# Attention and gated FFN in one kernel: q and k rows stacked by direct transfers between partitions, without a copy in memory

## The reference

```python
xn = layernorm(x)                       # x: (4, 512, 256), 4 batches
q, k, v = (xn @ W.T).reshape(B, T, 16, 16).transpose(0, 2, 1, 3) for W in (Wq, Wk, Wv)
w = softmax(causal(q @ k.T / sqrt(16)))
s = (w @ v).transpose(0, 2, 1, 3).reshape(B, T, 256) @ Wo.T
h = silu(xn @ Wg.T) * (xn @ Wu.T)       # 704 hidden, integer weights, zero point 128, a scale per row
g = silu(h @ Wd.T)
out = x + s * g
```

## Time and profile before

| | |
|---|---|
| median of 3 runs | 336.36 us (335.95 to 337.09) |
| profiled execution | 337.07 us |
| its span, first to last instruction | 335.2 us |
| TensorE / VectorE / ScalarE / GpSimd busy | 291.8 / 208.7 / 173.8 / 126.7 us |
| mean granted TensorE clock | 0.929 of full |
| moved by DMA | 31.41 MB, mean 94 GB/s |

### The profile page before, as it was taken

The page is one execution under the profiler, slowest core; times in us unless marked ns, Lnnn a source line. Parts: engine busy times, 40 slices in busy tenths (PEclk is TensorE's granted clock), DMA queues, the critical chain, the costliest instruction groups (busy, mean ns, idle before and its releaser), DMA issues.

```text
span 335.2 us, 5853 instructions
## 1 busy us (share of the span) xinstructions
PE 291.8 (87%) x2076; PEld 210.7 (63%) x2076; DVE 208.7 (62%) x714; ACT 173.8 (52%) x252; POOL 126.7 (38%) x227
## 2 busy tenths in 40 slices
PE   8798575999719999995997999999987999989983
PEld 8687443885515775892565666779553667747752
DVE  4994819686326866754385468494763699882305
ACT  3556327135426578931545464962661656774451
POOL 5108514043213679230215544450323366732130
PEclk9899958799978999997898599999999799998999
DMA  7936896006959000069266000025594400120001
GB/s 275 262 101 177 198 154 135 2 6 176 156 171 178 14 4 0 3 171 183 92 150 157 9 6 0 4 66 171 121 200 109 94 3 3 66 65 2 5 0 63
DMA packets 21632, 31.41 MB, mean 94 GB/s; under 512 B 2772, under 2 KB 10580, under 8 KB 21604
## 3 DMA queue, kind: packets, MB, share of 16 engines
q1 hardware_dynamic: 21188, 30.40, 38.5%
q10 hardware_dynamic: 416, 0.66, 0.5%
HBM read 20.20 MB, written 10.49 MB: 92 GB/s over the span
## 4 chain that ended last, share of the span: by engine, by line
PE 54%; DMA 23%; SPq 9%; DVE 7%; ACT 4%; issue 2%; POOL 0%; ACTq 0%; DVEq 0%
DMA qk_scratch<-hid 14%; PE ps L422 11%; PE ps L563 9%; PE ps L424 9%; PE ps L423 9%; PE ps L546 6%; PE ps L526 5%; DMA qp<-ctr 3%; SPq L372 3%; DMA qk_scratch<-xr 2%; DVE ps L976 2%; DMA kp<-qk_scratch 2%; ACT pt L760 2%; PE ps L573 2%; DMA pt<-in_woT 2%
## 5 line engine op out<-in xcount | busy, mean ns | idle before, releaser
L976 DVE CUSTOM_DVE_ANT_0 ps<-ps,maskt 128x512 f32<-128x512 f32 (+3 forms) x256 | 118.2, 521 | 38.7 <-PE ps L526 38.7
L824 POOL TENSOR_SCALAR_AFFINE_SELECT pt<-pt 128x256 f32<-128x256 f32 (+1 forms) x112 | 47.9, 443 | 127.3 <-ACT pt L760 126.2
L760 ACT ACTIVATE pt<-ps 128x1024 f32<-128x1024 f32 x80 | 79.9, 1028 | 23.3 <-PE ps L546 16.1
L546 PE MATMUL ps<-qp,kp 50*128 50x512 f32 (+3 forms) x256 | 37.0, 369 | 17.8 <-DVE hid L955 7.4
L526 PE MATMUL ps<-kp,qp 48*128 48x512 f32 (+3 forms) x256 | 36.3, 363 | 12.5 <-DMA kp<-qk_scratch 8.2
L800 POOL TENSOR_TENSOR hid<-hid 128x512 f32<-128x512 f32 x24 | 30.8, 1282 | 33.8 <-ACT hid L708 23.3
L422 PE MATMUL ps<-xh,guh 128*128 128x512 f32 x88 | 41.4, 470 | 2.1 <-DVE hid L955 2.1
L563 PE MATMUL ps<-pt,vt 128*32 128x256 f32 (+3 forms) x528 | 41.5, 458 | 1.7 <-POOL pt L824 1.5
L546 PEld LDWEIGHTS ps<-qp,kp 50*128 50x128 f32 x256 | 21.6, 196 | 31.0 <-issue 13.5
L700 ACT ACTIVATE hid<-ps,hsg 128x512 f32<-128x512 f32 (+1 forms) x24 | 16.4, 685 | 42.1 <-DMA qk_scratch<-hid 21.6
L526 PEld LDWEIGHTS ps<-kp,qp 48*128 48x128 f32 x256 | 21.9, 196 | 24.8 <-issue 21.5
(11 more groups left out here) (112 smaller groups left out, 482.5 us busy)
## 6 DMA issues: line engine op xcount, KB each, us to landing
qk_scratch<-hid SPq DMA_DIRECT2D x24, 256.0 KB
qp<-qk_scratch SPq DMA_DIRECT2D x14, 256.0 KB, 4.9
kp<-qk_scratch SPq DMA_DIRECT2D x14, 256.0 KB, 5.7
qp<-qk_scratch SPq DMA_DIRECT2D x18, 128.0 KB, 5.3
kp<-qk_scratch SPq DMA_DIRECT2D x18, 128.0 KB, 5.7
xr<-in_x SPq DMA_DIRECT2D x4, 512.0 KB, 4.5
out<-xr SPq DMA_DIRECT2D x8, 256.0 KB, 2.2
xin<-in_x SPq DMA_DIRECT2D x3, 512.0 KB, 7.7
```

The lines of the kernel that those rows point to most:

```text
L546: mm = nc.tensor.matmul(ps[:, banks[e], c:c + T - j * P], kp[part, place(b, half), col, j * P:(j + 1) * P], qp[part, place(b, half), col, ...
L760: nc.scalar.activation(pair(b, s), ps[:, b0:b1 + 1:b1 - b0, :], ACT.Exp, scale=SCALE).then_inc(exp_done, 1)
L824: mm = nc.gpsimd.affine_select(out=diag, in_=diag, compare_op=ALU.is_ge, fill=0.0, base=0, pattern=[[0, diag.shape[1]], [1, P]], channel_m ...
L976: mm = nc.vector.tensor_tensor_reduce(part, part, maskt[:, T - wide:], -1.0, TOP, ALU.add, ALU.min, mg[:, e, a // 2, i:i + 1])
```

## The change

The q and k weights are put in another column order, so that chunk g of `qk` is group g: 64 rows of q and 64 rows of k for four heads. From the staging tile, six DMAs between partitions write the stack at once: 64 staging partitions go to 32 partitions by two columns, each fourth partition of `qp` or `kp`. Of every four rows in `qp` three hold high, low, high, and in `kp` high, high, low; the fourth row is 0 in `qp` and 1 in `kp`. The rows of maxima go to partition 31 of every 32 in one DMA. All matmuls of both passes run over 64 rows. Since the first pass needs 0 where the second has the maxima, a DMA writes zeros there before a place is used again. `qp` and `kp` have 6 places of 4 heads, filled once by GpSimd. q and k get a staging tile `stg` of their own with two places, and the tanh no longer waits for transfers; `fth` is merged into `u` and `sdb` lies in `u`. `vt` is packed to 17 columns per head. The weights' split into high and low goes in three parts. All five orders are written anew.

```diff
-PAIRS = 6, ROWC = 3 * HD, KS = ROWC + 2
+PLACES = 6, VE = HD + 1
...
-            def store_qk(b, c):
-                half, which = c // 2, c % 2
-                w.need("qlo", qlo_done, 4 * b + c + 1)
-                if b >= 2:
-                    w.need(("pack", b % 2, half), pack_loaded[b % 2][half], 128 * (b // 2))
-                for s in range(2):
-                    sp.dma_start(qk_dram[b % 2, which, half, :, s], stage(b, c)[s]).then_inc(qk_stored[c], 16)
-
-            def stack_cols(b, half, which, cols, loaded):
-                w.need(("stored", 2 * half + which), qk_stored[2 * half + which], 32 * (b + 1))
...
+            def place_free(n):
+                if n < PLACES:
+                    w.need("rows", rows_set, 2 * (n + 1))
+                else:
+                    w.need("st", st_ready, 5 * (n - PLACES + 1))
+
+            def stack_hi(b, g):
+                n = NG * b + g
+                w.need("qhi", qhi_done, n + 1)
+                place_free(n)
+                if n >= PLACES:
+                    if n == PLACES:
+                        sp.wait_ge(ctr_zero, 1)
+                    sp.dma_start(qp[31::32, place(b, g)].bitcast(F32), ctr[:, 2, :].bitcast(F32)
+                                 ).then_inc(stacked[b % 2][g], 16)
+                hi = stage(b, g)[0]
+                for rows, src in ((qp[0::4], hi[0:64]), (kp[0::4], hi[64:P]), (qp[2::4], hi[0:64]), (kp[1::4], hi[64:P])):
+                    sp.dma_start(rows[:, place(b, g)].bitcast(F32), src.bitcast(F32)).then_inc(stacked[b % 2][g], 16)
+
+            def stack_lo(b, g):
+                n = NG * b + g
+                w.need("qlo", qlo_done, n + 1)
+                place_free(n)
+                lo = stage(b, g)[1]
+                for rows, src in ((qp[1::4], lo[0:64]), (kp[2::4], lo[64:P])):
+                    sp.dma_start(rows[:, place(b, g)].bitcast(F32), src.bitcast(F32)).then_inc(stacked[b % 2][g], 16)
 
             def c_rows(b, g):
                 n = NG * b + g
                 w.need("ct", ct_copied, n + 1)
-                for r in range(2):
-                    a = 2 * (g % 2)
-                    sp.dma_start(qp[64 * r + ROWC:64 * r + KS, place(b, g // 2), a:a + 2, :].bitcast(F32),
-                                 ctr[16 * r:16 * r + 16, n % 2, :].bitcast(F32)).then_inc(c_loaded[n % 2], 16)
+                sp.dma_start(qp[31::32, place(b, g)].bitcast(F32), ctr[:, n % 2, :].bitcast(F32)).then_inc(c_loaded[n % 2], 16)
...
             def chunk_hi(b, c):
                 w.need("qk", qk_ready, 4 * b + c + 1)
-                if b == 0 and c == 3:
-                    w.need("wl", wl_done, 2)
-                if b:
-                    w.need("hlo", hlo_done, HF * b)
-                    w.need("hlt", hlt_done, b)
                 if b and c >= 2:
-                    w.need(("stored", c - 2), qk_stored[c - 2], 32 * (b + 1))
-                nc.scalar.copy(stage(b, c)[0].bitcast(F32R), ps[:, bank_of("qk", b, c), :]).then_inc(qhi_done, 1)
+                    w.need(("stacked", b % 2, c - 2), stacked[b % 2][c - 2], stack_count(b, c - 2))
+                elif b:
+                    q, g = b - 1, (c if b == 1 else c + 2)
+                    w.need(("stacked", q % 2, g), stacked[q % 2][g], stack_count(q, g))
+                nc.scalar.copy(stage(b, c)[0], ps[:, bank_of("qk", b, c), :]).then_inc(qhi_done, 1)
...
             def gate_tanh(b, m):
                 w.need("gu", gu_ready, GUN * b + 2 * m + 1)
                 if m >= 2:
                     w.need("hlo", hlo_done, HF * b + m - 1)
+                elif b and m == 0:
+                    w.need("hlo", hlo_done, HF * b)
                 elif b:
-                    for c in (m, m + 2):
-                        w.need(("stored", c), qk_stored[c], 32 * (b + 1))
-                else:
-                    w.need("ones", kp_ones, 32)
+                    w.need("hlt", hlt_done, b)
...
+            def rows(_, n):
+                nc.gpsimd.memset(kp[:, n].bitcast(F32), 1.0).then_inc(rows_set, 1)
+                nc.gpsimd.memset(qp[:, n].bitcast(F32), 0.0).then_inc(rows_set, 1)
...
 TENSOR_ORDER (start)
-t:0:0:0 t:0:1:1 qk:0:0:0 qk:0:1:1 qk:0:2:2 qk:0:3:3 gu:0:0:0 gu:0:1:1 gu:0:2:2 gu:0:3:0 gu:0:4:1 gu:0:5:0 v:0:0:2
-m:0:0:01 m:0:1:34 m:0:2:56 v:0:1:7 m:0:3:01 gu:0:6:2 m:0:4:37 gu:0:7:4 m:0:5:56 gu:0:8:2 m:0:6:04 gu:0:9:1 gu:0:10:3
+t:0:0:0 t:0:1:1 qk:0:0:0 qk:0:1:1 qk:0:2:2 qk:0:3:0 gu:0:0:1 gu:0:1:3 gu:0:2:0 m:0:0:12 m:0:1:34 m:0:2:56 gu:0:3:7
+v:0:0:1 v:0:1:0 m:0:3:12 m:0:4:34 m:0:5:56 m:0:6:07 gu:0:4:1 gu:0:5:2 gu:0:6:3 c:0:0:1 gu:0:7:2 m:0:7:01 m:0:8:45
 SYNC_ORDER (after; units of batches 0 to 2)
+init4:0:0 loadx:1:0 pkh:0:0 pkl:0:0 pkl:0:1 pkh:0:1 pkh:0:2 pkl:0:2 pkh:0:3 pkl:0:3 loadres:0:0 crow:0:0 loadx:2:0
+crow:0:1 loadx:3:0 crow:0:2 pkh:1:0 pkl:1:0 pkh:1:1 pkl:1:1 crow:0:3 pkh:1:2 pkl:1:2 pkh:1:3 pkl:1:3 crow:1:0
+sout:0:0 sout:0:1 crow:1:1 loadres:1:0 crow:1:2 pkh:2:0 pkl:2:0 pkh:2:1 pkh:2:2 pkl:2:1 pkl:2:2 crow:1:3 pkh:2:3
 VECTOR_ORDER (start)
+init2:0:0 st:0:0 xn:0:0 xn:0:1 xn:0:2 xn:0:3 wlo:0:0 wlo:0:1 wlo:0:2 glo:0:0 xlo:0:0 xlo:0:1 wds:0:0 wol:0:0 bn:1:0
+wdl:0:0 qlo:0:0 qlo:0:1 bn:1:1 glo:0:1 qlo:0:2 qlo:0:3 bn:1:2 bn:1:3 gate:0:0 mom:1:0 maxa:0:0 maxb:0:0 maxa:0:1
```

More of the change, by code:

```diff
@@ L89 @@
+hhi:3:5 exp:3:4 fth:3:0 ccp:3:2 exp:3:5 zcp:3:0 exp:3:6 exp:3:7 exp:3:8 fth:3:1 exp:3:9 exp:3:10 ccp:3:3 exp:3:11
+exp:3:12 exp:3:13 zcp:3:1 exp:3:14 exp:3:15 exp:3:16 zhi:3:0 zcp:3:2 exp:3:17 exp:3:18 exp:3:19 zcp:3:3 zcp:3:4
+zhi:3:1 zhi:3:2
 """
 VECTOR_ORDER = """
-init2:0:0 st:0:0 xn:0:0 xn:0:1 xn:0:2 xn:0:3 wlo:0:0 glo:0:0 xlo:0:0 xlo:0:1 glo:0:1 wol:0:0 wds:0:0 qlo:0:0 qlo:0:1
-wlo:0:1 wdl:0:0 qlo:0:2 gate:0:0 qlo:0:3 bn:1:0 bn:1:1 bn:1:2 gate:0:1 bn:1:3 mom:1:0 gate:0:2 maxa:0:0 maxb:0:0
@@ L129 @@
+hid:3:0 mask:2:15 hlo:3:0 mask:2:16 mask:2:17 hid:3:1 mask:2:18 mask:2:19 hlo:3:1 hid:3:2 hid:3:3 hlo:3:2 hlo:3:3
+hid:3:4 hlo:3:4 mask:3:0 res:2:0 hid:3:5 mask:3:1 mask:3:2 mask:3:3 res:2:1 mask:3:4 mask:3:5 mask:3:6 mask:3:7
+mask:3:8 mask:3:9 mask:3:10 mask:3:11 mask:3:12 mask:3:13 mask:3:14 mask:3:15 mask:3:16 mask:3:17 mask:3:18
+mask:3:19
 """
 SYNC_ORDER = """
-init4:0:0 loadx:1:0 store:0:0 store:0:1 stackf:0:0 stackf:0:1 store:0:2 store:0:3 stack:0:0 stack:0:1 stack:0:2
-stack:0:3 loadres:0:0 loadx:2:0 crow:0:0 crow:0:1 store:1:0 store:1:1 stack:1:0 stack:1:1 loadx:3:0 store:1:2
@@ L409, in store_out @@
                              xr[:, 2 * n:2 * n + 2, :]).then_inc(out_stored, 16)
-            work = {"init4": load_first, "loadx": load_x, "loadres": load_residual, "store": store_qk,
-                    "stackf": stack_first, "stack": stack, "crow": c_rows, "sout": store_out}
+            work = {"init4": load_first, "loadx": load_x, "loadres": load_residual, "pkh": stack_hi, "pkl": stack_lo,
+                    "crow": c_rows, "sout": store_out}
             for kind, b, n, _ in SYNC:
@@ L513, in maxima @@
                 g, kk = divmod(m, 5)
-                half = g // 2
                 banks = take(("m", b, m))
-                if b == 0 and g == 0:
-                    w.need("first", first_pack, 128)
-                else:
-                    w.need(("pack", b % 2, half), pack_loaded[b % 2][half], 128 * (b // 2 + 1))
+                w.need(("stacked", b % 2, g), stacked[b % 2][g], stack_count(b, g))
                 both = [pair_blocks(kk, e) for e in range(2)]
@@ L524, in maxima @@
                         i = TT - 1 - j
[L525 to L527 removed]
+                        wide, part, col = (i + 1) * P, slice(64 * e, 64 * e + 64), a // 2
+                        mm = nc.tensor.matmul(ps[:, banks[e], c:c + wide], qp[part, place(b, g), col, i * P:(i + 1) * P],
+                                              kp[part, place(b, g), col, 0:wide], start=True, stop=True)
                 mm.then_inc(sm_ready, 1)
@@ L751, in exps @@
                 if n < PAIRS:
-                    w.need("wl", wl_done, 2)
+                    w.need("wl", wl_done, 3)
                     w.need("gul", gul_done, 2)
                     w.need("wol", wol_done, 1)
-                    for c in range(4):
-                        w.need(("stored", c), qk_stored[c], 32)
+                    w.need(("stacked", 0, 2), stacked[0][2], 96)
                 else:
@@ L849, in root @@
                     nc.gpsimd.tensor_scalar(shf[:], t, -1.0, None, ALU.mult).then_inc(shf_done, 1)
-            work = {"init3": constants, "sc": scales, "root": root, "mask": mask, "hid": hidden, "hlo": hidden_lo,
+            work = {"init3": constants, "rows": rows, "vones": value_ones, "sc": scales, "root": root, "mask": mask, "hid": hidden, "hlo": hidden_lo,
                     "res": residual}
```

295 lines of the change are left out of this document (133 added, 162 removed).

## The result

The change makes the kernel faster: 305.74 us (304.58 to 306.67) against 336.15 us before on the same chip, ratio 0.9096, 95% interval 0.9051 to 0.9142. That is 30.4 us; forecast were 18.2. The profiled execution's span is 304.9 us against 335.2.

A forecast was written before the change was run, and what follows sets the result against it. TensorE was taken as nearest the limit (busy 291.8 of 335.2 us), with 26.3 of its 43.4 idle us hanging on transfers, plus low clock. Terms summed to -18.2, from 337.1 to 318.9, stated as 318 us; range 302 to 336.

The forecast's parts named there:

- (a): TensorE's waits for stacked k rows, 8.2 us, all go but 1.2 before the first maxima: -7.0, bounds -8.2 to 0.
- (b): TensorE's waits through the gate vanish as the tanh no longer waits for transfers: -11.2, or -6 if something else delays it.
- (c): TensorE's 6.9 us of waits for rows of maxima shrink, rows still in SyncE's queue: -2, bounds -4 to +4.
- (d): TensorE work at the lower clock in four stretches partly returns to full clock: -8, bounds -11.5 to -2.
- (e): Start: weight splits in seven copies and a wait for the first bank delay TensorE: +2, bounds +0.7 to +5.
- (f): GpSimd's twelve fills of kp and qp end near 14, before they are needed: 0, or +2 with the cover gone.
- (g): From batch 1, ScalarE's copies of chunks 2 and 3 wait for groups 0 and 1 to land: +3, bounds 0 to +30.
- (h): TensorE runs into ScalarE's exponentials more often, their 4.9 us of waits doubling: +5, bounds 0 to +10.
- Rival 1: More comes back: no new waits and the clock in full, 304 us; chance 0.16 (below 310).
- Rivals 2, 3 and 5: Stalls only move, 330, chance 0.14; ScalarE's staging waits slow it, 346, 0.08; removed waits overlapped, nothing won, 0.05.
- Rival 4: Strided transfers to every fourth partition move badly, deciding near 14 us a group; 356 at 20 us; chance 0.04.

The follow-up runs named there:

- the two runs above: Kernel before with a staging tile of its own: 329.55 us, ratio 0.9918; kernel after with the tanh waiting again for staged groups: 337.0 us, ratio 1.0137.
- The runs with the link: Kernel after with q and k stores added and SyncE waiting for every landing: 362.52 us; waiting for the low parts' stores only: 336.84 us.
- the run with late fills: Kernel after with GpSimd's 12 fills of kp and qp moved behind the fills of vt and wdl and the scales: 296.28 us, ratio 0.8819.

## Why the prediction was right in direction, and 12 us short

**(a) k rows, -7.0.** Came as -8.2: no wait for `kp` is left.

**(b) The gate, -11.2.** Came in full. But its worth depends on the rest, as the two runs above show: alone on the old path 1 to 4.5 us, while a stronger tie put on the new path costs 31.

**(c) `ctr`, -2.** Came as -6.9, the whole term, outside my bounds (-4 to +4). This term was undersized. I blamed the landing on full DMA engines and counted up to 21 issues ahead. For the largest wait the landing was the greater part indeed, 1.8 of the 4.03 us being the queue; and the row of the next one (1.93 us at 56.66) went out 0.03 us after its copy. What I had wrong is how much of it would be left. Rows still stand in SyncE's queue, three of them 3.4, 1.5 and 6.0 us (copied at 85.39, 157.23 and 203.58), and TensorE waits for none: it has other work, 5.00 of the 5 us from 85 to 90 and 16.00 of the 16 from 200 to 216, and the DMA engines' share is 0.81 and 0.73 there, where it was 0.99. Whether the new order or the freer engines took the wait away isn't separated. The runs with the link show what the queue costs when SyncE stands for landings, which the change never makes it do for a store of q or k.

**(d) Clock, -8.** TensorE's busy time fell by 13.2 us. An estimate of the clock's part: in stretches of 2 us, busy time times what the granted clock lacks to 1.00 adds up to 19.2 us before and 8.7 after, so the clock gave back 10.5, and 2.7 aren't traced. I had allowed 11.5 at most, from four stretches, where the trace had 19.2 to give; and all this although the kernel after runs at the lower clock from 18 to 28:

```profile
18.00:28.00 10.00, 6.85 (x20) 5.46 (x21) 9.40 (x17) 3.66 (x5) 0.00 (x0) 0.50 0.19 56
...
78.00:99.00 21.00, 20.54 (x133) 14.45 (x131) 18.17 (x74) 12.24 (x19) 10.70 (x27) 1.00 0.64 144
```

The second row is the stacking of batch 1, the counterpart to 88 to 97 in the earlier trace rows: TensorE stands for 0.46 us of 21.

**(e) The start, +2.** Without the block, 14.86 instead of 13.78 and a wait of 1.26 us for the first bank: 2.3. Right, seen in the run with late fills (the weights' low part in seven took 2.16 us instead of 1.22, 0.9 of my 1.2 to 1.5). The first projection of gate and up starts only 1.0 us later there (21.95 instead of 20.96), because the old start ran at the lower clock from 14.78 to 18.18.

**(f) The fills, 0.** This step failed. I costed the 12 fills as work of an engine that has time, and looked for who waits for their results. What they cost is what they keep VectorE from: 8.2 us of start, 9.4 us in all with the clock. Nothing in the earlier trace rows shows a block, because the old fill of `vt` (3.51 to 5.30) was over before the first tensor_scalar at 5.90. My bound was +2.

**(g) The new wait of the chunk copies, +3.** ScalarE's wait for `kp<-stg` is 1.5 us in three times, and TensorE doesn't feel it. 0 instead of 3; I forecast 10 to 25 us for the row itself.

**(h) What is late next, +5.** TensorE's waits for exponentials fell from 4.9 to 2.7 us (2.2 and 0.5) instead of doubling, outside my bounds (0 to +10). The allowance had no row behind it.

The idle terms add up: -8.2 - 11.2 - 6.9 - 2.2 + 8.1 (7.4 and 0.7 at the start) = -20.4, and 3.3 in many small waits stand against it, 1.8 of them for VectorE's maxima. With -13.2 of busy time that is the 30.3. Two errors hid each other: the fills cost 9.4 more and the rest brought over 20 more than I said. Without the fills' block the result, 296.3, lies outside my range (302 to 336).

Rival 1 came nearest, all waits gone and the clock back, 304: its number is met because of the fills. Rivals 2, 3 and 5 fell. Rival 4 fell too: a group goes out in six issues of about 0.60 us, 3.8 us in all, close to the forecast's 4.1 and far from 14:

```profile
80.45 0.59 SPq L389 DMA_DIRECT2D qp<-stg  x1
...
83.65 0.60 SPq L397 DMA_DIRECT2D kp<-stg  x1
84.35 0.55 SPq L389 DMA_DIRECT2D qp<-stg  x1
```

SyncE's issues set the pace there; from 28 to 33 the DMA engines were nearly full as well, at 0.92 with 205 GB/s. Of the prediction's two estimates for a group, 2.4 us by the writes or 4.1 as now, these rows are near the second, but no run measures the rate by itself. Only half of the old stack loads that the 190 GB/s came from write 32 partitions (L382); the others write 16 (L384).

**What stays open.** The old orders were never run with the new path, nor the new ones with the old kernel's chunks, so the part of the new order in the gain isn't separated. Nor is it known why the block by fills was broken once without a pause. The slower runs with the link say what a standing SyncE costs in the new order, not what it cost in the old one.

## What to carry to other kernels

A wait on an in-order DMA queue is paid by what stands behind it; find the small urgent transfer in the queue before the large one. When work is given to an idle engine, ask not only who waits for it but whom it shuts out while it runs, and put long fills where the neighbour has none of the blocked kind. A stall that is tied to several others (gate, stack, maxima) can be worth little alone: freeing the gate won 1 to 4.5 us where all changes together won 30, a third of it clock.

## What the runs showed of the hardware

- VectorE's tensor_scalar on fp32 and int32 in SBUF doesn't run beside a fill by GpSimd: 8.22, 3.92 and 0.97 us instead of 0.17. Its tensor_tensor (0.16 us) and scalar_tensor_tensor (1.75 us) run beside one undisturbed. Beside that scalar_tensor_tensor a small tensor_scalar of GpSimd took 2.01 us instead of 0.25, once.
- Waiting for one landing of 256 KB in SyncE's queue takes 1.7 us for a high part (23.8 us in 14 times) and 2.1 for a low one (29.5 in 14); 60.9 us of such standing cost 50.7, 33.2 cost 25.
- How long a row of maxima takes to land goes with how full the DMA engines are: in the kernel before 3.56 us for the one at 52.85, at a share of 0.65, and 6.95 for the one at 149.86, at 0.99.
- The 128 KB transfers from 64 partitions to each fourth partition cost SyncE 0.60 us each (0.43 for the last stack load in the earlier trace rows), and no matmul after waited for one. An issue of 8 KB cost ScalarE 0.62 us.
